# A block of adaLN attention with a differential softmax on one core: GpSimd takes the first steps of VectorE's exponentials, and tokens are turned by VectorE and DMA in place of TensorE

## The reference, cut to what matters

```python
h = layernorm(x) * (1 + ca) + sa
q, k, v = h @ Wq.T, h @ Wk.T, h @ Wv.T          # 32 heads of 8 for q and k, 16 of 16 for v
attn_w = softmax((q * 8 ** -0.5) @ k.T)          # fp32, [B, 32, T, T]
aw = attn_w[:, :, 0] - lam * attn_w[:, :, 1]     # by pairs of heads
a = rms_norm(aw @ v) * subln_w * (1 - LAMBDA_INIT)
x = x + ga * (a @ Wo.T)
h = layernorm(x) * (1 + cb) + sb
x = x + gb * (h @ ternary(Wf).T)
```

## Time and profile before

| | us |
|---|---|
| median of three runs | 3610.86 (3609.04 to 3613.66) |
| the profiled execution's own time | 3607.35 |
| its span, first to last instruction | 3605.5 |
| ScalarE busy in the span | 3534.4 |
| VectorE busy in the span | 2588.9 |
| GpSimd busy in the span | 338.0 |

### The profile page before, as it was taken

The page is one execution under the profiler, slowest core; times in us unless marked ns, Lnnn a source line. Parts: engine busy times, 40 slices in busy tenths (PEclk is TensorE's granted clock), DMA queues, the critical chain, the costliest instruction groups (busy, mean ns, idle before and its releaser), DMA issues. The chain is left out here.

```text
span 3605.5 us, 76890 instructions
## 1 busy us (share of the span) xinstructions
PE 3405.9 (94%) x32302; PEld 799.1 (22%) x32302; DVE 2588.9 (72%) x3808; ACT 3534.4 (98%) x2808; POOL 338.0 (9%) x229
## 2 busy tenths in 40 slices
PE   8999999999899999999999999999999999989998
PEld 5222112122122222222222222222221222211222
DVE  6687878863578687776367768677547888878886
ACT  5999999999999999999999999999999999999998
POOL 3010101010010100101001010100100000000001
PEclk9999999999999999999999999999999999999999
DMA  6111110111101111101111001111012110010000
GB/s 196 28 32 39 32 31 22 35 39 33 38 21 42 48 35 40 50 23 33 36 47 50 25 31 36 40 49 36 20 31 63 45 37 22 17 30 16 20 22 26
DMA packets 103700, 136.90 MB, mean 38 GB/s; under 512 B 9916, under 2 KB 88716, under 8 KB 103340
## 3 DMA queue, kind: packets, MB, share of 16 engines
q1 hardware_dynamic: 102524, 131.01, 12.9%
q10 hardware_dynamic: 816, 0.79, 0.1%
HBM read 72.50 MB, written 59.19 MB: 37 GB/s over the span
## 5 line engine op out<-in xcount | busy, mean ns | idle before, releaser
L1146 ACT ACTIVATE probs<-ps 128x1536 f32<-128x1536 f32 (+1 forms) x2732 | 3497.4, 1670 | 15.5 <-PE ps L1263 13.9
L1291 PE MATMUL ps<-probs,values 128*32 128x512 f32 x14600 | 2047.9, 606 | 4.9 <-DVE wmod_sb L1644 2.4
L1263 PE MATMUL ps<-queries,keys 25*128 25x512 f16 x7680 | 1003.9, 385 | 160.6 <-ACT probs L1146 142.0
L1263 PEld LDWEIGHTS ps<-queries,keys 25*128 25x128 f16 x7680 | 249.8, 91 | 1947.3 <-ACT probs L1146 1861.5
L1291 PEld LDWEIGHTS ps<-probs,values 128*32 128x32 f32 x14600 | 300.2, 108 | 416.9 <-issue 410.5
L1623 DVE TENSOR_SCALAR d_y<-ps 128x512 f32<-128x512 f32 x240 | 165.6, 690 | 295.4 <-PE ps L1263 284.7
L1708 DVE STREAM_TRANSPOSE seg_t<-ps 128x512 f32<-128x512 f32 x127 | 91.0, 716 | 356.9 <-PE ps L1291 356.4
L1060 POOL TENSOR_TENSOR seg_rs<-seg_ms,neg_half 128x16 f32<-128x16 f32 x64 | 185.7, 2901 | 1506.1 <-DVE seg_ms L1721 1506.1
L1640 DVE SCALAR_TENSOR_TENSOR wmod_sb<-wmod_sb 128x1024 f32<-128x1024 f32 x204 | 249.6, 1224 | 6.3
L1644 DVE SCALAR_TENSOR_TENSOR wmod_sb<-wmod_sb,gates 128x1024 f32<-128x1024 f32 x204 | 249.5, 1223 | 6.0
L1642 DVE SCALAR_TENSOR_TENSOR wmod_sb<-wmod_sb,d_y 128x1024 f32<-128x1024 f32 x204 | 249.3, 1222 | 5.3
(11 more groups left out here) (181 smaller groups left out, 1690.9 us busy)
## 6 DMA issues: line engine op xcount, KB each, us to landing
v_scr<-a_v SPq DMA_DIRECT2D x16, 1024.0 KB, 5.6
values<-v_scr SPq DMA_DIRECT2D x29, 512.0 KB
queries<-q_scr SPq DMA_DIRECT2D x116, 96.0 KB
keys<-k_scr SPq DMA_DIRECT2D x116, 96.0 KB
e_x<-in_x_dram SPq DMA_DIRECT2D x18, 512.0 KB, 5.2
attn_scr<-seg_o SPq DMA_DIRECT2D x254, 32.0 KB
e_attn<-attn_scr SPq DMA_DIRECT2D x31, 256.0 KB, 3.6
out_dram<-e_y SPq DMA_DIRECT2D x15, 512.0 KB, 3.3
```

What stands on the lines that cost most here:

```text
L1146: nc.scalar.activation(probs[:, s % PRING, at, :], ps[:, base + at.start:base + at.stop:at.step, :], ACT.Exp, scale=1.0 / SQUARE).then_inc ...
L1263: last = nc.tensor.matmul(ps[:, score_bank(n), :], keys[buf][at, u * P:(u + 1) * P], queries[buf][at, tc * CH:(tc + 1) * CH], start=True, ...
L1291: last = nc.tensor.matmul(pv[row:row + VW, :], values[buf][:, n % SEG_BANKS // HEADS, j // 2, :], probs_of(n), start=(i == 0), stop=(i == ...
```

## The change

- **Blocks.** Two blocks in every segment but the first, the last and the second half of each batch's turn: 231 blocks, 462 banks. `D_UNITS` becomes units 3 and 5, and 8 and 10. The number of slots stays 2732.
- **GpSimd computes** round, fraction and exponent, bank by bank (`whole_part`, three instructions of 128x512), as soon as VectorE has read the bank. VectorE keeps the read and the four steps of the polynomial; the first of them waits for `g_done` of both banks. Each block place has tiles of its own (`d_y`, `gates`; `g_y`, `g_n`). The constants of the polynomial are fitted anew.
- **Turning.** The steps a 0, a 1, e 2 and e 3 are no longer made on TensorE, nor evacuated by VectorE. `norm_apply` writes `normed` by squares, VectorE turns 32x32 squares in one instruction of 128x1024 (`turn_normed`), SyncE issues 16 DMAs within SBUF that move the squares to their places (`turn_squares`), and GpSimd scales and shifts both halves in place (`scale_turned`). This holds for 27 jobs; the opening's four jobs and the last job stay as they were.
- **Places.** The remaining steps of a job are spread over the body, sums are split into four tasks, GpSimd gets an order of its own (`pool_order_of`), and its splits no longer wait for `d_done`.

```diff
+    A_FIRST_MADE, E_MADE = 2, (0, 1, 4, 5)
...
+        if 0 < b < B - 1 and not turn:
+            spread = [[NB + 14 * (PIECES * j + p) // 5 for p in range(PIECES)] for j in range(A_MADE + len(E_MADE))]
+            put("a", body + NC, [(), ()] + spread[0:4] + spread[6:8])
+            put("e", body - GP, spread[4:6] + [(), ()] + spread[8:10])
...
-    D_UNITS = ((4, 6), (8, 10))
+    D_UNITS = ((3, 5), (8, 10))
     D_AT = (14, 15)
-    D_LINKS = 6
+    D_LINKS, G_LINKS = 3, 2
...
-        return 2 if sum(light.get(step, 3) for step in steps) <= 5 and not normed else 1
+        return 2
...
-    SHARE_COST = (695, 1230, 695, 1225, 1225, 1225, 1225)
+    NORM_WAIT, POWER_WAIT, STATS_AT, APPLY_AT = 3300, 1300, 1, 3
+    SHARE_COST = (1300, 1300, 1300, 1300)
+    POOL_LAG = 4000
...
+    SUMS_COST = (1060, 600, 950, 1250)
+    SUMS_AT = 3
...
+    TURN_WAIT = 12000
+    G_COST = (900, 1270, 900)
...
+                        for job in turned_behind(body, s):
+                            turn_squares("e", job)
+                        if s == SEGS - 1 and body + 1 < (B - 1) * GP:
+                            turn_squares("a", body + 1 + NC)
...
+            def turn_squares(kind, job):
...
+                sp.wait_ge(square_turned, TURN_OF[kind, job] + 1)
+                for row in range(P // 32):
+                    for col in range(P // 32):
+                        src = turned[32 * col:32 * col + 32, :, 32 * row:32 * row + 32]
+                        dst = hT[32 * row:32 * row + 32, :, :].rearrange("p c (n t) -> p (c n) t", n=BPC)[:, :, 32 * col:32 * col + 32]
+                        sp.dma_start(dst, src).then_inc(turn_done, DMA)
...
+            def scale_turned(kind, job, c):
...
+                if c == 0:
+                    pool.wait_ge(turn_done, (TURN_OF[kind, job] + 1) * SQUARES * DMA)
+                nc.gpsimd.tensor_scalar(hT[:, c, :], hT[:, c, :], cols_sb[:, first + 1, c, m:m + 1], cols_sb[:, first, c, m:m + 1], ALU.mult, ALU.add).then_inc(done, 1)
...
+            def whole_part(n, part):
...
+                if part == 0:
+                    pool.wait_ge(d_read, D_ORDER[n] + 1)
...
+                    link.then(nc.gpsimd.tensor_scalar(whole, y, ROUND, -ROUND - SHIFT, ALU.add, ALU.add))
+                elif part == 1:
+                    link.then(nc.gpsimd.tensor_tensor(y, whole, y, ALU.subtract))
+                else:
+                    nc.gpsimd.tensor_scalar(whole.bitcast(mybir.dt.int32), whole, BIAS + SHIFT, 2.0 ** 25, ALU.add, ALU.mult).then_inc(g_done, 1)
+                    pool.wait_ge(g_done, 2 * share + half + 1)
...
+            def turn_normed(applied, job):
...
+                V.transpose(turned[:, :, :].rearrange("p n f -> p (n f)"), normed[:, :, :].rearrange("p n e -> p (n e)")).then_inc(square_turned, 1)
...
                 if part == 0:
-                    dve.wait_ge(d_read, 2 * (share + 1))
-                    link.then(V.tensor_scalar(d_n, y, ROUND, -ROUND, ALU.add, ALU.add))
+                    dve.wait_ge(g_done, 2 * share + 2)
+                    if k:
+                        dve.wait_ge(pv_done, OPEN + k * NB)
+                    link.then(V.scalar_tensor_tensor(out, f, -POLY[0], f, ALU.add, ALU.mult))
```

More of the change, by code:

```diff
@@ L323, in evacuation, with slot_at, sums_parts @@
     def evacuation(s, kind, i):
-        return 815 if kind == "a" and i < 2 or kind == "e" and i in (2, 3) else 850 if kind == "m" else 700
-    def first_slot(kind, job, i, start):
-        return next((s for s in range(start, ALL_SLOTS) if any(step == (kind, job, i, 0) for step in STEPS_AT[s])), ALL_SLOTS)
+        return 850 if kind == "m" else 700
+    def slot_at(clock):
+        return next((s for s in range(ALL_SLOTS) if STARTS[s + 1] > clock), ALL_SLOTS)
+    SUMS_COST = (1060, 600, 950, 1250)
+    SUMS_AT = 3
+    def sums_parts(k):
+        return 4 if k % 2 or k == ALL_SEGS - 2 else 3
     def order_of(b):
@@ L418, in adaln_diff_attention @@
+    TURNS = [("a", NC)]
+    for body in range(B * GP):
+        for _, kind, job, i, p in sorted((u, *step) for u, step in steps_of(body).items()):
+            if kind == "e" and i == 1 and p == PIECES - 1:
+                TURNS.append(("e", job))
+        if body + 1 < (B - 1) * GP:
+            TURNS.append(("a", body + 1 + NC))
+    TURN_OF = {turn: n for n, turn in enumerate(TURNS)}
     LAST_JOB = (B - 1) * NC
@@ L1044, in _ @@
             a_power(NC)
+            for c in range(EC):
+                scale_turned("a", NC, c)
             for b in range(B):
@@ L1056, in _ @@
                         e_power(task[0])
[L1057 removed]
+                    elif what == "rest":
                         rows = slice(0, P if task[0] % 2 else 64)
@@ new lines, in segment_sums @@
+                link = Chain(dve, s_chain, k // 2 * links + second * S_LINKS + (0, 1, 2, 4)[part])
+                here, other = slice(64 * second, 64 * second + 64), slice(64 - 64 * second, 128 - 64 * second)
+                rows = slice(0, P if second else 64)
+                if part == 0:
+                    dve.wait_ge(pv_done, OPEN + (k + 1) * NB)
+                    V.transpose(seg_t[:, :, :].rearrange("p c d -> p (c d)"), pv).then_inc(pv_read, 1)
+                    dve.wait_ge(pv_read, k + 2)
+                    link.then(V.reciprocal(seg_r[:, :], seg_t[:, :, VD]))
+                elif part == 1:
+                    link.then(V.scalar_tensor_tensor(seg_w[:, :, :], seg_t[:, :, 0:VD], coef[:, 0:1],
+                                                     seg_r[:, :].rearrange("p (c o) -> p c o", o=1).broadcast_to([P, NQ, VD]), ALU.mult, ALU.mult))
+                elif part == 2:
+                    link.then(V.tensor_copy(seg_w2[here, :, :], seg_w[other, :, :]))
+                    link.then(V.tensor_tensor(seg_d[here, :, :], seg_w[here, :, :], seg_w2[here, :, :], ALU.add))
+                else:
@@ L1897, in _ @@
                         a_apply(task[0])
+                    elif what == "turn":
+                        turn_normed(*task)
                     elif what == "gates":
```

276 lines of the change are left out of this document (150 added, 126 removed).

## The result

The changed kernel takes 4016.89 us (median of four runs, 4008.12 to 4026.41) beside 3612.14 of the kernel before in the same session: 1.1122 times as long, 95% interval 1.1096 to 1.1149. Forecast were 3591 and a range to 3680. The profiled execution took 4016.7, its span is 4014.9. All that follows asks where 405 us come from.

The account below looks back on a forecast made before the run. ScalarE, busy 98%, was taken as the bound: 3607.35 - 22.7 (54 banks at 0.42) + 3 (collisions) = 3587.7, given as 3591 since the runs' median stands 3.5 higher. Range 3583 to 3680.

Parts of the forecast that it names:

- What bounds it, and the price of a bank: ScalarE, busy 98%, is the bound; each of 54 banks taken from it is worth 0.42 us, together -22.7 us.
- the +3 for collisions: Where GpSimd and VectorE meet, 3 us added for some reads just over the allowance.
- TensorE's 82 us count as nothing: Turning of 27 jobs leaves TensorE, 82 us of work; worth nothing in time, since TensorE follows ScalarE.
- SyncE and the turn: 16 DMAs a turn take 9.7 us to issue; hidden, since GpSimd's scale comes 12 us behind the turn.
- the turn is late: Rival: 128-byte DMA runs at 0.073 us a packet delay GpSimd's next block; 70 us, time 3658; chance 0.05.
- GpSimd's part, 2.8 us per bank: GpSimd's three instructions per bank take 2.8 us with hand-overs (2.6 to 3.6), 1300 us in all; room enough.
- The second block, 8.5 us needed of 11.6: From second block's last read to its group: 0.7 read, 2.8 GpSimd, 4 * 1.25 steps; margin 3.1 to 4.4 us, no stall.
- The two engines shut each other out: Rival: VectorE's two-input SBUF instructions and GpSimd's SBUF-reading ones exclude each other for full length; 3675 us; chance 0.22.
- The price of +86: Exclusion stretches sums before unit 5's read; 1.6 us lost in each of 54 odd segments, +86 us.
- the steps of second blocks come late as well, 1 us in each of 111: Addition to the exclusion case: late polynomial steps of second blocks would make the time 3785 us.
- the lower bound of 3583: Low end of the forecast's own range: banks worth 24.4 us by the means, and 5 us of stalls gone.

Follow-up runs that it names:

- write_short: Changed kernel with GpSimd's round, fraction and exponent replaced by memsets of 640, 1024 and 640 columns, which read nothing; result not computed: 3596.8 us.
- vector_picked: Changed kernel with round, fraction and exponent back on VectorE, 209 blocks, statistics and their application two slots later; turning kept: 3615.33 us, ratio 1.0015 to the kernel before.
- write_long: Changed kernel with GpSimd's round, fraction and exponent replaced by memsets of the same lengths, which read nothing; result not computed: 3775.8 us.
- round_mult: Changed kernel with GpSimd's rounding as an addition and a multiplication by one, shorter but leaving out the rounding itself: 3690.1 us.
- forms: Kernel before, with eleven forms of GpSimd instruction of 128x512 set three times at its program's start, to time each alone: 3647.1 us.
- round_twice: Changed kernel, computing the same, with GpSimd's rounding as two instructions, each a multiplication by one and an addition: 3914.6 us.

## Why the prediction was wrong

**What bounds it, and the price of a bank.** Right. In write_short, with all parts of the change but GpSimd's reads and lengths, 54 banks at 0.42 give 3587.7 in the sum and 3591 with the median; it took 3596.8. Its lateness in all is 52.7 us beside 43.2 before, so the +3 for collisions should have been about +10.

**TensorE's 82 us count as nothing.** Right that they don't shorten the program (vector_picked); by busy time they were 52. **SyncE and the turn.** Right in the time, less so in the cover: GpSimd's scale waited for its DMAs 38.2 and 35.0 us in 12 of 54 times, up to 19.7, so 12 us weren't always enough. In write_short it waited still longer (85.5 and 52.3 us, 20 times, up to 22.4) and the time stood only 6 us above the forecast. The rival "the turn is late" had its packets wrong, as the text suspected: twice the packets take 13.6% of a span for 12.9, which makes about 0.011 us for each packet more, where it had 0.073.

**GpSimd's part, 2.8 us per bank.** This is the step that failed first. "I take 2.8 with hand-overs, as one input is like the cast" took 0.68 for an instruction of one input from the cast; the rounding took 1.92 by itself, a sum of 3.85 per bank free, outside the bounds of 2.6 to 3.6. The bounds were drawn from two rows that share neither operation nor form with it. The exponent, which has a multiplication, is 0.62, near the 0.68 taken. The row that could have warned me doesn't exist; that the range of forms was unknown could have been said.

**The second block, 8.5 us needed of 11.6.** The second failure, and the one that carries the loss: 0.69 + 13.43 = 14.1. Of the 5.6 us more, 3.0 are the start behind the read, 2.0 GpSimd's instructions, 0.5 the steps. I had costed each bank as if GpSimd were free when its read ends; that needs a bank to take less than the 3.6 us between reads. 3.85 doesn't, and 4.76 doesn't even beside the 4.33 between reads that the change itself has. The prediction closed this with "So as long as the engines run freely, no stall", and they don't.

**"The two engines shut each other out".** The mechanism is shown (write_long, and the steps' lengths), with most of its signs: the third step at 1.82, `seg_d` at 0.57, and 69.3 us of TensorE's waits for reads; `seg_w` stayed at 0.48. The price of +86 was for reads behind the sums. What it had as an aside, that "the steps of second blocks come late as well, 1 us in each of 111", is the main loss: 295.7 / 111 = 2.7 us each. It was wrong in the place: a late read shows two slots on, so that of unit 5 at unit 6, and the slots there are late by 19.2 us in all, 13.3 in the segments that follow an odd one, where +86 was put. TensorE waited longer for the reads of second blocks (43.6 us) than of first ones (25.7). round_mult, where reads are left and the length is gone, took 3690, close to the rival's 3675, but that is luck: 63.0 us of its lateness stand at unit 2 and 34.5 at unit 6. Even so the 0.22 it was given was too low for a rule that a row had already borne out, with 1300 us of GpSimd's instructions put beside VectorE's.

**That the two failures meet.** The forecast took them apart. From write_short on, exclusion alone costs 93 us, length alone 179, both together 420, where the forecast's bound for what the engines cost each other was 86. Two slips of the text are small beside this: by its own terms the lower bound of 3583 comes to 3581.5, and the third rival's 3658 lacks the 3.5 us that the others have.

## What to carry to other kernels

An instruction whose form of operations no row shows has no neighbour in the trace: time it by itself before its length carries a date, and on GpSimd try a form with a multiplication in it. When work goes to an engine that shuts out the one it is taken from, add up the time of both between the first read and the date; moving pieces within that stretch helped the whole in none of three tries here. A stage that serves items one after another needs to be shorter than their spacing, not than the whole time to the date.

## What had not been expected of the hardware

A pair of additions, or of an addition and a subtraction, costs GpSimd 1.92 us for 128x512, where a pair with a multiplication costs 0.62 and a single addition 1.50 (forms). A copy took 0.61 and a memset 0.52 there.

TensorE's clock falls behind the stalls. Around the stall in front of the segment shown, first the group that waited, then windows of 2 us (columns: PE, PEld, DVE, ACT, POOL busy, granted clock, DMA):

```profile
1331.65 0.81 PE L1404 MATMUL ps<-probs,values 128*32 128x512 f32 x2 [3.89 <-DVE wmod_sb L1747]
...
1329.00:1331.00 2.00, 0.00 (x0) 0.00 (x0) 1.95 (x2) 0.59 (x1) 0.00 (x0) 1.00 0.00 0
1331.00:1333.00 2.00, 1.35 (x8) 0.19 (x8) 0.50 (x1) 0.00 (x0) 0.00 (x0) 0.74 0.03 8
1333.00:1335.00 2.00, 2.00 (x18) 0.41 (x14) 1.46 (x3) 1.07 (x1) 0.00 (x0) 0.50 0.00 0
1335.00:1337.00 2.00, 2.00 (x18) 0.41 (x19) 1.38 (x3) 1.60 (x3) 0.61 (x1) 0.91 0.00 0
```

TensorE stood still for 3.9 us, waiting for the block's last step, and the granted clock, 1.00 (2.4 GHz) before, fell to 0.50 (1.2 GHz) just as it had a late group and late scores to catch up with; from 1333 to 1335 us it was 0.50 throughout. In that window and the next TensorE is busy all the time and ScalarE only 1.07 and 1.60 of 2.00 us. So this stall seems to cost more than its own length. Over the span the granted clock is 0.941 for 0.998 before, and it falls with the loss: 0.956 in round_twice, 0.972 in write_long, 0.984 in round_mult, 0.995 in write_short. How much of the 405 us is the clock's wasn't tried apart from the stalls that bring it about, and stays open.
